# Expert outputs added into four tables in HBM, a scatter waiting for the second one before it

## What is computed

```python
topk_w, topk_ids = _grouped_topk(x @ gate_w, bias)     # 6 of 64 experts for each of 2048 tokens
pos = place of the token among those that chose the same expert
valid = pos < CAP                                      # CAP = 48 rows of an expert; later ones are dropped
h = silu(buf @ w_gate) * (buf @ w_up)                  # 64 experts, 48 rows each, 256 -> 96
out = h @ w_down                                       # 96 -> 256
y = segment_sum(out * w, tok)                          # the sum over a token's experts
x = layernorm(x + y + shared(x))
```

## Time and profile before

| | |
|---|---|
| median of 3 runs | 1066.99 us (1065.76 to 1068.21) |
| the profiled execution | 1058.62 us |
| its span | 1056.8 us, 1.8 us less than its time |
| busy in the span | PE 90%, DVE 68%, ACT 49%, POOL 41% |
| first TensorE work of the expert stage | 942.2 us |
| first scatter to `sums` | 952.1 us |
| last scatter landed | 1008.9 us |
| end of the span | 1056.8 us |

### The profile page before, as it was taken

The page is one execution under the profiler, slowest core; times in us unless marked ns, Lnnn a source line. Parts: engine busy times, 40 slices in busy tenths (PEclk is TensorE's granted clock), DMA queues, the critical chain, the costliest instruction groups (busy, mean ns, idle before and its releaser), DMA issues.

```text
span 1056.8 us, 17584 instructions
## 1 busy us (share of the span) xinstructions
PE 951.3 (90%) x5456; PEld 734.0 (69%) x5456; DVE 722.6 (68%) x1789; ACT 520.8 (49%) x1139; POOL 430.6 (41%) x390
## 2 busy tenths in 40 slices
PE   8999996978999999999977889999999999639955
PEld 6888775756788877777766667888778777516522
DVE  5988862757767776766747878676777777445527
ACT  4012133545556656666655656556565665216503
POOL 3877882234342422215256545243323140325511
PEclk9999998989999999999999999999999999869979
DMA  8786776422334121212132434431212114899587
GB/s 249 233 282 207 237 262 170 138 91 71 114 98 121 47 80 44 68 36 68 53 112 82 126 92 118 111 96 42 76 34 68 37 39 118 199 248 290 158 297 280
DMA packets 137946, 139.80 MB, mean 132 GB/s; under 512 B 18643, under 2 KB 107855, under 8 KB 137856
## 3 DMA queue, kind: packets, MB, share of 16 engines
q1 hardware_dynamic: 87264, 102.53, 31.8%
q10 hardware_dynamic: 43872, 29.50, 9.6%
q0 software_dynamic: 6720, 6.66, 2.2%
HBM read 88.54 MB, written 65.14 MB: 145 GB/s over the span
## 4 chain that ended last, share of the span: by engine, by line
PE 69%; DVE 11%; issue 6%; DMA 4%; POOL 4%; SPq 3%; ACT 2%; ACTq 1%; POOLq 0%; DVEq 0%
PE s_ps L1201 16%; PE ring L1211 10%; PE o_ps L1231 10%; PE o_ps L1228 8%; PE ring L1250 6%; PE s_ps L1180 4%; PE ring L1180 4%; SPq L821 2%; PE s_ps L1305 2%; DVE neg_max L1416 2%; PE ring L1319 1%; PE ring L1241 1%; PE o_ps L1180 1%; POOL prods L875 1%; PE s_ps L1204 1%
## 5 line engine op out<-in xcount | busy, mean ns | idle before, releaser
L1045 ACT ACTIVATE probs<-s_ps,neg_max 128x128 f32<-128x128 f32 (+7 forms) x256 | 189.6, 741 | 117.3 <-DVE neg_max L1416 107.1
L1201 PE MATMUL s_ps<-kt,qt_hi 128*128 128x512 f32 (+3 forms) x768 | 231.0, 382 | 5.7 <-issue 2.4
L1416 DVE TENSOR_REDUCE neg_max<-s_ps 128x1 f32<-128x128 f32 (+7 forms) x256 | 191.6, 751 | 55.7 <-PE s_ps L1204 54.1
L1211 PE MATMUL ring<-ident,probs 128*128 128x128 f32 x1152 | 177.5, 277 | 19.9 <-ACT probs L1045 10.0
L1201 PEld LDWEIGHTS s_ps<-kt,qt_hi 128*128 128x128 f32 x768 | 137.5, 192 | 51.4 <-issue 29.4
L945 ACT ACTIVATE pt_hi<-ring 128x512 fp32r<-128x512 f32 x168 | 100.1, 596 | 141.9 <-PE ring L1211 139.2
L890 POOL TENSOR_TENSOR ot_lo<-ot_raw,ot_hi 128x512 fp32r<-128x512 f32 x52 | 66.7, 1282 | 240.8 <-ACT ot_hi L945 240.8
L1350 DVE TENSOR_TENSOR pt_lo<-ring,pt_hi 128x512 fp32r<-128x512 f32 x168 | 115.6, 689 | 68.3 <-ACT pt_hi L945 66.0
L1211 PEld LDWEIGHTS ring<-ident,probs 128*128 128x128 f32 x1152 | 129.4, 143 | 44.5 <-issue 23.9
L1231 PE MATMUL o_ps<-pt_hi,v 128*128 128x512 f32 x336 | 144.2, 430 | 0.0
L895 POOL TENSOR_TENSOR qt_lo<-q_raw,qt_hi 128x512 fp32r<-128x512 f32 x64 | 82.3, 1287 | 132.0 <-ACT qt_hi L945 131.7
(11 more groups left out here) (220 smaller groups left out, 1566.0 us busy)
## 6 DMA issues: line engine op xcount, KB each, us to landing
qk_rows<-prods SPq DMA_DIRECT2D x80, 256.0 KB, 2.9
q_raw<-qk_rows ACTq DMA_DIRECT2D x128, 128.0 KB, 3.0
inv_row<-inverses SPq DMA_DIRECT2D x64, 256.0 KB, 3.5
sums<-blank SPq DMA_DIRECT2D x17, 768.0 KB
fsum<-sums SPq DMA_DIRECT2D x48, 256.0 KB, 8.7
wexp<-in_L_ffn_w_gate_dram SPq DMA_DIRECT2D x32, 192.0 KB, 4.5
wexp<-in_L_ffn_w_up_dram SPq DMA_DIRECT2D x32, 192.0 KB, 5.0
wexp<-in_L_ffn_w_down_dram SPq DMA_DIRECT2D x32, 192.0 KB, 6.5
```

The lines of the kernel that those rows point to most:

```text
L1045: act.activation(probs[:, u % 2, h, 0:blocks(u) * P], s_ps[:, n % 2, score_cols(n)], ACT.Exp, bias=neg_max[:, n % 8:n % 8 + 1], accum_out= ...
L1201: pe.matmul(s_ps[:, n % 2, c + a:c + e], q[qp], k[kp][:, a:e], start=(qp == kp == 0), stop=(qp == 1 and not last))
L1211: ins = pe.transpose(bank(s)[:, h * P:(h + 1) * P], probs[:, u % 2, h, j * P:(j + 1) * P], ident[:, :])
L1416: dve.tensor_reduce(neg_max[:, n % 8:n % 8 + 1], s_ps[:, n % 2, score_cols(n)], AX_X, ALU.max, negate=True).then_inc(max_ready, 1)
```

## The change

The six tables become four, and the residual has no tensor of its own: it is stored in table 0, whose token rows are no longer zeroed. A row of rank r goes to table r modulo 4, so that ranks 4 and 5 share the tables 0 and 1 with ranks 0 and 1, and everything in table 0 is added to the residual. The scatters add to what is there in place of writing over it. Two rows of one token in the same table come from experts at least four numbers apart, so at least two pairs apart; each scatter waits for the landing of the second one before it. The last stage loads four tables and nothing else.

```diff
-TABLES = K
+TABLES = 4
-Z_HOMES = 26
@@ SyncE, zeros: three tables, and the spare rows of all four
-                sp.dma_start(table_rows[i * P:(i + 1) * P, :, :],
-                             blank[:, 0:M].rearrange("p (a r) -> p a r", a=1).to_broadcast([P, TABLES, M])
+                sp.dma_start(table_rows[i * P:(i + 1) * P, 1:, :],
+                             blank[:, 0:M].rearrange("p (a r) -> p a r", a=1).to_broadcast([P, TABLES - 1, M])
@@ SyncE, the residual's store
-                    sp.dma_start(z_rows[i * P:(i + 1) * P, :], z_sb[:, :]).then_inc(z_stored, 16)
+                    sp.dma_start(sums[i * P:(i + 1) * P, :], z_sb[:, :]).then_inc(z_stored, 16)
@@ SyncE, the residual's loads
-            sp.wait_ge(dn_ready, Z_HOMES)
-            for c in range(FINAL):
-                sp.dma_start(fz[:, c, :], z_of_rows[:, c, :]).then_inc(fsum_loaded[c], 16)
@@ GpSimd
             pool.wait_ge(experts_blank, 16 * (TILES + 1))
+            pool.wait_ge(z_stored, 16 * TILES)
             for n in range(PAIRS):
                 if n in CHUNK_AT:
                     pool.wait_ge(slots_known, CHUNK_AT[n] + 1)
                 pool.wait_ge(erow_ready, n + 1)
+                if n >= 2:
+                    pool.wait_ge(erow_sent[(n - 2) % EB], sent_before[(n - 2) % EB] + 16 * ((n - 2) // EB + 1))
                 pool.indirect_dma_start(
                     sums[:, :], bass.IndirectOffsetOnAxis(ap=goal_u[0:USED, n:n + 1], axis=0),
-                    erow[0:USED, n % EB, :], None, bounds_check=TABLES * TABLE - 1, oob_is_err=False
+                    erow[0:USED, n % EB, :], None, bounds_check=TABLES * TABLE - 1, oob_is_err=False, compute_op=ALU.add
                 ).then_inc(erow_sent[n % EB], 16)
@@ TensorE, even chunks
-                pe.wait_ge(fsum_loaded[c], 16 * (TABLES + 1))
-                pe.matmul(sum_rows(c), ident[:, :], fz[:, c, :], start=True, stop=False)
+                pe.wait_ge(fsum_loaded[c], 16 * TABLES)
                 for a in range(TABLES):
-                    ins = pe.matmul(sum_rows(c), ident[:, :], fsum[:, c, a, :], start=False, stop=(a == TABLES - 1))
+                    ins = pe.matmul(sum_rows(c), ident[:, :], fsum[:, c, a, :], start=(a == 0), stop=(a == TABLES - 1))
@@ VectorE, rank modulo 4, behind line 1570
+                    step(dve.tensor_scalar(turned[:, 0:b - a], rank[:, 0:b - a], float(TABLES), -float(TABLES),
+                                           ALU.is_ge, ALU.mult))
+                    step(dve.tensor_tensor(rank[:, 0:b - a], rank[:, 0:b - a], turned[:, 0:b - a], ALU.add))
@@ VectorE, odd chunks
-                dve.wait_ge(fsum_loaded[c], 16 * (TABLES + 1))
-                add(dve.tensor_tensor(fsum[:, c, 0, :], fsum[:, c, 0, :], fz[:, c, :], ALU.add))
+                dve.wait_ge(fsum_loaded[c], 16 * TABLES)
                 for a in range(1, TABLES):
                     add(dve.tensor_tensor(fsum[:, c, 0, :], fsum[:, c, 0, :], fsum[:, c, a, :], ALU.add))
```

More of the change, by code:

```diff
@@ L323, in build @@
     v_rows = nc.dram_tensor("v_rows", (VS * P, G * D), F32, kind="Internal").ap()
-    z_rows = nc.dram_tensor("z_rows", (TOKENS, M), F32, kind="Internal").ap()
     sums = nc.dram_tensor("sums", (TABLES * TABLE, M), F32, kind="Internal").ap()
@@ L449, in build @@
         rank = sb("rank", [P, MOST], F32, exp)
+        turned = sb("turned", [P, MOST], F32, exp)
         exp.close()
@@ L460, in build @@
         fout = sb("fout", [P, FINAL, PER_ROW * M], F32, fin)
-        fz = sb("fz", [P, FINAL, PER_ROW * M], F32, fin)
         fin.close()
@@ L663, in build @@
                       for a in range(TABLES)]
-        z_of_rows = z_rows.rearrange("(p c r) m -> p c (r m)", p=P, c=FINAL)
         out_rows = of.rearrange("(p c r) m -> p c (r m)", p=P, c=FINAL)
```

## The result

The changed kernel takes 1076.66 us (median of 7 runs, 1071.92 to 1079.43), the kernel before beside it 1064.83 us: a ratio of 1.0106, 95% interval 1.008 to 1.0132, or 9 to 14 us slower. The profiled execution took 1076.66 us with a span of 1074.8, 18 us more than the profiled one of before.

The account below looks back on a forecast made before the run. TensorE's expert matmuls up to the last scatter, then DMA table loads, were taken as the bound. 8.0 (wait, ranks) + 9.6 (addition) - 10.8 - 2.2 = +4.6 on 1066.99 gave 1071.6 us, range 1060.5 to 1087.5.

Parts of the forecast that it names:

- Loads and sums: Last stage: 16 of 48 table loads go, 10.8 us, and three of six VectorE additions behind the last landing, 2.2 us.
- Ranks: Two more small VectorE steps per chunk; two chunks stand ahead of the first `hid_t` copy, adding 0.8 us on the path.
- The wait with d = 0: Expert stage: scatters chained two back, adding themselves costing nothing, make the last landing 7.2 us later.
- d: What adding costs a scatter over a plain write; estimated 0.6 us, forecast band 0.4 to 1.1.
- r: Time from release to start of a GpSimd scatter, taken as 0.8 us for release by a landing too.
- L: Scatter's start to landing: about 6 us up to 970, 3.3 to 986, 2.4 behind that.
- 16 d with d = 0.6: Addition's cost along the scatter chain, 15 times by the steps and once by the last landing: 9.6 us.
- the dear rival: Addition dear in the crowd or on GpSimd, d from 1.1 up; at 1.5, +19 us, 1086 us; 20%.
- an addition for nothing: Rival: scatter addition costs nothing that shows, d under 0.18; -5.0 us, 1062.0 us; 25%.
- The rival that hides it all: Expert stage hides the scatter chain, steps under 3.5 us; 1056 to 1058 us; 3%, within another rival's 25%.
- the doubled packets: Second rival: adding only doubles the DMA engines' packet time, d about 0.26; -0.8 us, 1066.2 us; 20%.
- -5.0 + 16 d: Whole change in us, wait and ranks less removed loads and sums, plus addition; breaks even at d = 0.31 us.

Follow-up runs that it names:

- the later pair of single runs: No edit: the kernel before and the changed kernel, run once each in the series of the changed kernel's second profile; 1062.79 and 1074.11 us.

## Why the prediction was right, and where its reasons were not

Forecast +4.6 us, 1071.6, range 1060.5 to 1087.5, slower at 53%. Measured +11.8 by the medians. The sign and the mechanism were right, the terms of what is removed and of the ranks came out, and the two large ones, the wait and the addition, were too small.

- **Loads and sums, 10.8 + 2.2 = 13.0 us.** Measured: last landing to end 34.8 us against 47.5 and 47.9, 12.7 to 13.1. The loads take 25.5 us, forecast 25.6. SyncE's issue and VectorE stayed under the DMA, as said.
- **Ranks, 0.8 us.** The new steps stand on the path ahead of the first `hid_t` copy, two per chunk, 0.2 us each. From the expert stage's first weight load on TensorE to the first scatter it is 10.7 us in the changed kernel (943.17 to 953.86) and 9.9 in the one before (942.21 to 952.11): 0.8 us, as forecast.
- **The wait with d = 0, 7.2 us: wrong by half.** This is the step that failed. It measured 14.8 us with four tables, the ranks' 0.8 not in it since the stage is counted from the first scatter, and 16.8 with six, where the residual's loads crowd the end of the stage as well (DMA share 0.84 in 1004 to 1012, against 0.16 with four). The assumed r of 0.8 us holds, and so do the first two crowded steps (6.9 and 7.7 us in the changed kernel with plain writes, 7.0 forecast). What failed is L afterwards, the landing time behind the crowd: the next three steps there took 5.5, 4.7 and 5.2 us, 15.4 in all, where I had 4.4, 3.25 and 3.25, with 2.5 us of extra for crowds later on. The landings that set them took 4.65, 3.81 and 4.39 us, not the 3.6 and 2.45 of the undisturbed kernel. The late weights and slot rows are called up by progress and moved with the stage they slowed. And I had no pauses of GpSimd: the one before the twentieth scatter was in the timeline of before, 3.5 us of idle time, and I passed over it since it cost nothing there. The 15 steps there take 68.3 us and not 59.9: 0.6 in the two crowded ones, 4.5 in the next three, 3.3 in the last ten, of which the pause before the twentieth scatter, 2.7 us beyond a restart, is most. Removing the weights takes away half of the wait's cost.
- **16 d with d = 0.6: the form was right, the size was not.** d is 1.05 us; 14.0 us of stage is 13.3 d, not 16. That part of it falls into steps that pauses fill anyway is my guess; no run separates it. Of my 0.26 for packets and 0.3 for the read, 0.53 was found behind the instruction, near their sum, but split otherwise: the packets' own time has grown by 0.44. The missing 0.51 is GpSimd's, which I had put with the dear rival and not in the forecast. So idle landings take 3.5 us where I had said 3.0 to 3.1, and the last scatter lands at 1040 and not near 1027.
- **The sum.** 8.0 + 9.6 - 13.0 = +4.6 was forecast. The stages give 28.8 + 0.8 - 12.9 = +16.7, the profiled executions, means of two (1075.4 and 1060.05), +15.3, the medians +11.8. The median of before, 1064.83, lies above both of its profiles (1058.62 and 1061.48), that of after does not, hence the gap; for the size the interval of 9 to 14 us counts, and the later pair of single runs, 11.3 apart, fits it. The forecast was low, its range held. That -5.0 + 16 d with the measured d gives +11.8, the very difference of the medians, is luck: -5.0 was really about +3 to +8, and 16 was too much.

The rivals: an addition for nothing was given 25% and -5 us; run by itself it is +5 us, so even its price was wrong, by the same failed step. The rival that hides it all was summed wrongly (-13.0 + 0.8 + up to 1.6 leaves 1054.8 to 1056.4, not 1056 to 1058), which changes nothing, since both lie below the range. By the rule of the Trainium skill's page "Collectives: The Full Stack" (the bandwidth ceiling) d would have been the doubled packets, 0.26 us; measured, the part behind the instruction is twice that, the packets' time grows 2.7 times, and the fixed part on GpSimd isn't in the rule, so the trace doesn't bear it out as a price for a small scatter. The expert stage doesn't hide the wait: TensorE is done with the pairs some 16 us before the last landing.

## What to carry to other kernels

A wait for the landing of work k instructions back puts a ceiling on the rate, k in (landing + restart), and the ceiling must clear the pace by enough to make up for every pause: here, with plain writes, two back cleared it by some 4% where the DMA idles and lost 15 to 17 us of stage, three back lost under 4. Look in the timeline of before for pauses that are made up at once; they cost nothing until the slack they are made up from is gone. And read a landing time under the load that will run beside it, which may itself be late because of the wait.

## What the runs showed of the hardware

An adding indirect scatter from GpSimd takes 1.45 us of its time where the plain one takes 0.94, for 56 rows as for 112, and 112 rows of 1 KB land 3.5 to 3.6 us after the start, not 2.52, where no other load is under way; in 986 to 996, beside few other loads, their packets hold the 16 DMA engines 0.70 us and not 0.26. With one every 1.76 us and none waited for, adding cost the kernel under 7 us in 1060.

Beside the loads of weights and slot rows a plain scatter takes 5.6 to 6.9 us to land in the kernel before, and 2.5 where the DMA idles. From a semaphore's release to the start of GpSimd's scatter it is 0.8 us, whether `erow` or a landing releases it, and 0.30 us between two scatters that wait for nothing.

GpSimd pauses before the twentieth scatter in all runs with plain writes. Where nothing waits it is 3.5 us of idle time each time, 2.7 of them beyond the usual 0.8 behind its `erow`. It comes at the same scatter and not at the same time, but it isn't bound to the instruction: with additions of 112 rows, and the same number of instructions, the longest pause stands before the eleventh scatter in both runs without a wait (1.64 us, 0.74 before the twentieth), with additions of 56 rows before the eighteenth (1.59 us, none before the twentieth). So its place goes with what the scatters carry. What it is no run shows.
